# Second edge layer of a graph kernel: the softmax pieces two steps later, weighing and summing 14 and 16 steps behind the scores

## The reference

```python
# layer 0: attention with scores from Q and K
h = relu(layernorm(x))
Q, K, V = h @ Wq, h @ Wk, h @ Wv                       # 8 heads of 32
score = einsum('ehd,ehd->eh', K[src], Q[dst]) / sqrt(32) + edge_bias
attn  = softmax of score over the edges with the same dst
out   = segment_sum(attn * V[src], dst) @ Wp + bp
x     = x + layer_norm2(h1 + ffn(h1)),  h1 = layer_norm1(h + out)
# layer 1: attention with scores from two numbers per node and head
h = relu(layernorm(x)) @ W_lin + b_lin
feat = (h @ W_gat).reshape(N, 8, 32)
el, er = sum(feat * attn_l), sum(feat * attn_r)
e   = leaky_relu(el[src] + er[dst], 0.2)
a   = softmax of e over the edges with the same dst
out = leaky_relu(segment_sum(a * feat[src], dst) + gat_bias, 0.01)
x   = x + h + out
```

## Time and profile before

| | us |
|---|---|
| median of 3 runs | 7108.03 |
| lowest and highest | 7077.17, 7123.16 |
| the profiled execution | 7178.5 |
| its span, first to last instruction | 7176.6 |
| edge phase of layer 0 in it, about | 450 to 3150 |
| edge phase of layer 1 in it | 4276 to 6943 |
| mean granted TensorE clock in it, as a share of 2.4 GHz | 0.813 |

### The profile page before, as it was taken

One profiled execution on the slowest core, in us unless ns is written; L12 is line 12 of the kernel. 1 busy time (PEld: TensorE's weight loads), 2 busy tenths in 40 slices (PEclk: granted clock), 3 DMA queues, 4 the chain that ended last, 5 costly groups with the idle time before them and its releaser, 6 DMA issues. The chain is left out here.

```text
span 7176.6 us, 117024 instructions
## 1 busy us (share of the span) xinstructions
PE 5739.4 (80%) x24138; PEld 4403.4 (61%) x24138; DVE 4976.7 (69%) x12562; ACT 3482.2 (49%) x10958; POOL 3679.5 (51%) x4022
## 2 busy tenths in 40 slices
PE   8967777777777777779999948878788787888888
PEld 5545555555555555558999946666666666666666
DVE  4567888778888888886777736656566565665677
ACT  3356666666666666653333324444444444444440
POOL 1155555555555555534444455555555555655533
PEclk9978899889999999899999966666666666666669
DMA  5688888888988888872222235556556555665549
GB/s 182 202 248 268 271 280 279 266 264 280 286 274 272 274 271 278 264 235 80 85 85 85 84 105 167 165 162 166 168 163 168 161 161 162 170 166 163 163 142 296
DMA packets 849682, 1428.35 MB, mean 199 GB/s; under 512 B 123167, under 2 KB 628851, under 8 KB 849140
## 3 DMA queue, kind: packets, MB, share of 16 engines
q0 software_dynamic: 200192, 634.41, 31.1%
q1 hardware_dynamic: 543298, 511.88, 24.4%
q10 hardware_dynamic: 105650, 276.43, 10.0%
HBM read 1079.50 MB, written 342.73 MB: 198 GB/s over the span
## 5 line engine op out<-in xcount | busy, mean ns | idle before, releaser
L825 PE MATMUL bank<-ev,oh 128*128 128x264 f32 x7040 | 2557.0, 498 | 78.9 <-DVE ev L1284 60.6
L517 POOL DMA_INDIRECT Gf<-ft_tab,srcs x1564 | 1594.0, 1019 | 1154.7 <-DVE ev L1284 704.5
L517 POOL DMA_INDIRECT Gf<-kv_tab,srcs x1564 | 1508.0, 964 | 1308.7 <-DVE ev L1284 757.8
L825 PEld LDWEIGHTS bank<-ev,oh 128*128 128x128 f32 x7040 | 1619.8, 245 | 388.3 <-DVE ev L1284 88.3
L825 PE MATMUL bank<-qs,oht 128*128 128x256 f32 x3520 | 1077.3, 433 | 496.5 <-DVE prod L1193 245.5
L1284 DVE TENSOR_TENSOR ev<-Gf,ex 128x528 f32<-128x528 f32 x1760 | 1231.0, 699 | 2.1 <-ACT ex L686 1.3
L825 PE MATMUL bank<-Gf 128*128 128x128 f32 (+3 forms) x6284 | 1195.3, 343 | 4.5 <-ACT Gf L574 3.3
L825 PEld LDWEIGHTS bank<-qs,oht 128*128 128x128 f32 x3520 | 662.0, 209 | 770.9 <-issue 600.0
L614 ACT ACTIVATE absd<-lane,dlocs 128x128 f32<-128x128 f32 x3520 | 1112.8, 387 | 3.6 <-DVE bms L1159 3.5
L825 PEld LDWEIGHTS bank<-Gf 128*128 128x128 f32 x6284 | 936.1, 192 | 171.4 <-issue 98.7
L825 PEld LDWEIGHTS bank<-erq,oht 128*128 128x128 f32 x3520 | 735.1, 282 | 207.6 <-issue 157.7
(11 more groups left out here) (154 smaller groups left out, 5853.9 us busy)
## 6 DMA issues: line engine op xcount, KB each, us to landing
sums<-acc ACTq DMA_DIRECT2D x440, 528.0 KB
qs<-q_tab SPq DMA_DIRECT2D x880, 128.0 KB
oht<-dst_tab SPq DMA_DIRECT2D x880, 128.0 KB
qs<-dst_tab SPq DMA_DIRECT2D x880, 128.0 KB
Gf<-sums SPq DMA_DIRECT2D x196, 132.0 KB, 2.2
kv_tab<-Gf SPq DMA_DIRECT2D x98, 260.0 KB, 2.1
Gf<-in_x SPq DMA_DIRECT2D x196, 128.0 KB, 2.2
Gf<-kv_tab,srcs POOLq DMA_INDIRECT x1564
```

The lines of the kernel that those rows point to most:

```text
L517: pool.indirect_dma_start(out=rows[layer][:, m % SLOTS[layer], k, :], out_offset=None, in_=tab, in_offset=bass.IndirectOffsetOnAxis(ap=src ...
L825: return nc.tensor.matmul(o, a, r, start=first, stop=end)
```

## The change

In layer 1 alone (`LATE = (0, 2)`), the pieces of the softmax of block A move from steps 0 to 4 to steps 2 to 6 of the next turn, on DVE, ACT and PE. One piece stays: `scores_turned`, the transposition of S, is still in step 0. `links_turned` moves from step 5 to step 7, and the ACT part of the links from step 6 to step 0 of the turn after. Weighing and `agg` are 14 steps behind the scores in place of 12, `add` 16 in place of 14, and the stores 17 in place of 15. The ring of one-hots has twelve groups in layer 1; the two new ones lie in `prod`. One wait of ACT for its own `rm_made` is added, and the edge phase of layer 1 has one more turn at its end. Layer 0 keeps its order.

```diff
-OHG = 10
+OHG = (10, 12)
+BACK = (12, 14)
+LATE = (0, 2)
...
+        def group(B, g):
+            k = (B.n * 4 + g) % OHG[B.layer]
+            return oh[:, k, :, :] if k < OHG[0] else prod[:, k - OHG[0], :, :].rearrange("p k (a n) -> p (k a) n", n=P)
         def onehot(B, s):
-            return oh[:, (B.c * 4 + s // 2) % OHG, 2 * (s % 2):2 * (s % 2) + 2, :]
+            return group(B, s // 2)[:, 2 * (s % 2):2 * (s % 2) + 2, :]
...  ScalarE
-                wait(act, E_["agg"], B.c * ST + 2 * g + 2 - 2 * OHG)
+                wait(act, E_["agg"], B.c * ST + 2 * g + 2 - 2 * OHG[B.layer])
...
             def first_node(B):
+                if B.layer == 1:
+                    act.wait_ge(E_["rm_made"], B.c - 1)
...
-                        if s == 1 and A.live:
+                        if s == late + 1 and A.live:
                             row_values(A)
-                        if s == 2 and A.live:
+                        if s == late + 2 and A.live:
                             rescale(A)
-                        if s == 4 and A.live:
+                        if s == late + 4 and A.live:
                             factors(A)
-                        if s == 4 and B.live:
+                        if s == late + 4 and B.live:
                             link_rows(B)
-                        if s == 6 and B.live:
-                            links(B)
-                            if B.on(1).live:
-                                first_node(B.on(1))
+                        K, k = step_at(B, s - late)
+                        if k == 6 and K.live:
+                            links(K)
+                        if s == 6 and B.on(1).live:
+                            first_node(B.on(1))
...
-                        C, r = step_at(B, s - 15)
+                        C, r = step_at(B, s - BACK[layer] - 3)
...
-                for b in range(NB + 2):
+                for b in range(NB + 2 + layer):
...  TensorE (scores_turned(A) stays at s == 0)
-                        C, r = step_at(B, s - 12)
+                        C, r = step_at(B, s - BACK[layer])
                         if C.live:
                             agg(C, r)
-                        if s == 0 and A.live:
+                        if s == late and A.live:
                             row_values(A)
...  the same for columns, maxima_turned, rescale (1, 2, 3) and links_turned (5)
...  VectorE
-                        V_, v = step_at(B, s - 12)
-                        W_, w = step_at(B, s - 14)
+                        V_, v = step_at(B, s - BACK[layer])
+                        W_, w = step_at(B, s - BACK[layer] - 2)
...
-                        if s == 3 and A.live:
+                        if s == late + 3 and A.live:
                             below_maximum(A)
-                        if s == 6 and A.live:
-                            rescaled(A)
+                        if w == 0 and W_.live:
+                            rescaled(W_)
...
-                        if s == 0 and A.live:
+                        if s == late and A.live:
                             chunk_scans(A)
-                        if s == 2 and A.live:
+                        if s == late + 2 and A.live:
                             whole_scans(A)
...
-                        if s == 1 and A.live:
+                        if s == late + 1 and A.live:
                             row_scans(A)
```

More of the change, by code:

```diff
@@ L190, in build @@
         erq = sb("erq", [P, ST, H])
-        oh = sb("oh", [P, OHG, 4, P])
+        oh = sb("oh", [P, OHG[0], 4, P])
         oht = sb("oht", [P, ST, SPAN])
@@ L618, in onehots @@
                 act.wait_ge(E_["ohd"], 16 * B.c + 4 * g + 4)
-                wait(act, E_["agg"], B.c * ST + 2 * g + 2 - 2 * OHG)
-                act.activation(oh[:, (B.c * 4 + g) % OHG, :, :].rearrange("p c n -> p (c n)"),
+                wait(act, E_["agg"], B.c * ST + 2 * g + 2 - 2 * OHG[B.layer])
+                act.activation(group(B, g).rearrange("p c n -> p (c n)"),
                                absd[:, :, :].rearrange("p c n -> p (c n)"), ACT.Relu, scale=-1.0,
@@ L706, in edge_phase @@
             def edge_phase(layer):
-                at = {}
+                at, late = {}, LATE[layer]
                 def turn(B):
@@ L936, in edge_phase @@
             def edge_phase(layer):
+                late = LATE[layer]
                 def turn(B):
@@ L944, in turn @@
                             spread(layer, C, r)
-                        C, r = step_at(B, s - 12)
+                        C, r = step_at(B, s - BACK[layer])
                         if C.live:
                             agg(C, r)
-                        if s == 0 and A.live:
+                        if s == late and A.live:
                             row_values(A)
-                        if s == 1 and A.live:
+                        if s == late + 1 and A.live:
                             columns(A)
-                        if s == 2 and A.live:
+                        if s == late + 2 and A.live:
                             maxima_turned(A)
-                        if s == 3 and A.live:
+                        if s == late + 3 and A.live:
                             rescale(A)
-                        if s == 5 and B.live:
+                        if s == late + 5 and B.live:
                             links_turned(B)
@@ L1302, in edge_phase @@
             def edge_phase(layer):
-                at, landed = {}, {}
+                at, landed, late = {}, {}, LATE[layer]
                 def turn(B):
```

## The result

| | before | after |
|---|---|---|
| median of 3 runs, us | 7108.03 | 7010.25 |
| lowest and highest | 7077.17, 7123.16 | 7003.86, 7016.96 |
| the profiled execution | 7178.5 | 7010.25 |

The changed kernel takes 0.9869 of the time before, 95% interval [0.9838, 0.9899]: 98 us or 1.3% less. I had forecast 220 us. The sign is right, and the size is less than half of what I said. The forecast's own range, 6740 to 7040 us, takes 7010 in, since its upper end stands for only a third of the forecast gain.

What follows compares the result with a forecast made beforehand. The prediction took layer 1 to be bound by PE, starved at full clock by DVE's wait for the scan. 7178.5 - 225 + 5 = 6958.5 us profiled, or 7108 - 220 = 6888 us median; own range 6740 to 7040, whole range 6660 to 7130.

Steps and rivals of the forecast that it cites:

- PE, starved by DVE's wait for S: Layer 1's bound: PE idles 4.5 us per block, 3.4 us of it waiting for scans that DVE starts late.
- something I can't explain: At one block's scan, DVE starts 4.06 us after the transposition's record ends, though it waits for nothing else in the code.
- So the wait for a PE that is merely behind goes away: At `chunk_scans`, moved to step 2: DVE needs only what PE did two sums earlier; wait falls from 579.1 to under 100 us.
- I price a block in which PE never starves: Layer 1: 3.0 us per step at half clock, 2.4 at full, giving 22.3 us per block, 225 us less in all.
- the standstill moves: Rival, chance 0.25: PE's signals are held whatever DVE does, so waits move elsewhere; gain 0 to 0.5 us per block, 7080 us.
- the forecast's own rule: Layer 1's block is 24.0 us at half clock, less 0.25 us for each us at full clock.
- ACT's copies: ACT is busy for 44% of layer 1's stage, so its idle time covers the moved copies; costed at nothing.
- the ring: One-hot ring of twelve groups: margin between ACT and PE grows from two steps to four; nothing is paid.
- the later weighing: Slots are freed two steps later, gathers' lead shrinks from some 24 steps to 22; cost taken as zero.
- The full-clock rival: Rival, chance 0.12: PE, no longer starved, keeps 2.4 GHz for most of a block; 19.2 us per block, 6551 us.
- the slower one: Rival, chance 0.18: round trips meet a PE that is behind, so it idles later; 25.5 us per block, 7237 us.
- The drain of two steps: End of layer 1: two more steps drain after the last scores, 2 x 2.4 = 5 us.

Runs made afterwards that it cites:

- a_weigh_only: Changed kernel with the softmax pieces back at steps 0 to 4, only weighing, sums and ring moved, on a faster chip: 0.9998 of before, 18.86 us per block.
- set c: Runs on one slower chip, where the kernel before took 7107.58 us; the changed kernel repeated there took 7033.56 us, ratio 0.9891.
- The three controls: The changed kernel run again unaltered on three slower chips: 7023.49, 7033.56 and 7147.48 us, ratios 0.9899, 0.9891 and 0.9946 to the kernel before.
- c_weigh_only: Changed kernel with the softmax pieces back at steps 0 to 4, only weighing, sums and ring moved, on a slower chip: 1.0016 of before, 24.64 us per block.
- a_pause: Changed kernel with a memset that GpSimd waits for behind each pair of layer 1's gathers: 7378.54 us, ratio 1.0400, 27.45 us per block.
- a_half: Changed kernel with only the first of each span's two gathers in layer 1: 6460.32 us, 19.04 us per block.
- a_direct: Changed kernel with two plain loads of 128 rows in place of each span's two indirect gathers in layer 1: 6407.27 us, 18.72 us per block.
- c_busy: Changed kernel with plain loads in place of layer 1's gathers and two memsets behind each, keeping GpSimd busy: 6432.95 us, 18.91 us per block.
- after: The changed kernel as first profiled, against the kernel before: 7010.25 us, 0.9869 of the time before, 23.95 us per block of layer 1.

## Why the prediction was right in sign and wrong in size

**The bound.** "PE, starved by DVE's wait for S" described the trace but not its cause. I saw that a typical wait began with PE's backlog, and put the rest aside as something I can't explain. Against the rival I set that "the first 3 us of the wait are plain PE backlog". On a chip that holds no signal, the old order of these pieces has 104.1 us of waits there (a_weigh_only), about 1 us per block. PE is then busy for 93% of the stage, and GpSimd's gathers, at 1.32 us each for 14.2 per block, give 18.8 us per block where 18.86 was measured. Which of the two is the bound there isn't shown: with plain loads, which take GpSimd 559 ns, the block is still 18.7 us.

**The failed step** is what follows on "So the wait for a PE that is merely behind goes away", namely "I price a block in which PE never starves", with 22.3 us per block drawn from it. The wait at the scan did go, from 579.1 us to too little to be listed. But PE's idle time stayed, at 4.72 us per block, and the block is 23.95 us. DVE depends on PE at four points of a block's softmax and at two in every step, and a held signal stops it at whichever comes next. That is the rival "the standstill moves", which I gave 0.25, at the places that I had named for it: `add`, `el_er` (at `sred`) and `whole_scans`, together in 109 waits, one per block. Their longest are 5.0 to 7.1 us and their means 2.8 to 4.6 us. I sized it at 0 to 0.5 us per block, and 0.90 was measured (0.73 in set c). So the mechanism was the rival's, and the time lies between its price and the forecast's. POOL's wait for slots fell by 114 us, where I had named 200.

My line for being wrong was a block above 24 us. The three controls gave 24.12, 23.88 and 24.50, so the 23.95 of the first profile lies on it. That the time fell into the forecast's range is the width of the range and no support for its mechanism.

**What was gained** is PE's busy time, 1.09 us per block, less 0.19 us more of idleness. The same work was done at a mean clock of 0.68 in place of 0.64. Why the full clock lasts longer when the standstills fall in five places is not shown by any run. Had the forecast's own rule held (a quarter of a us back for each us at full clock), the rise of 0.04 in the clock, which is 0.08 x 24 = 1.9 us more at full clock, would give 0.5 of the 0.9 us; the rest is unaccounted for.

**The base.** The cut stage gave 24.36 us per block in place of 24.85. It made the forecast's gain 0.5 us per block smaller, so without this slip I would have been further off. That was luck.

**The other pieces.** ACT's copies, the ring, the added wait and the later weighing were costed at nothing. c_weigh_only confirms it for all but the copies (1.0016), for which there is no run. The full-clock rival did not happen (0.68, not 0.8), nor did the slower one, whose sign was a clock near 0.5. DVE does wait longer at `acc` for a PE that is behind, 116.6 us against 43.4 us in the whole stage before, but `acc` is none of the three round trips that this rival was about. At those the waits for a held signal cover what a backlog might add, so its mechanism is neither shown nor excluded. The drain of two steps is lost in the spread.

**What stays open:** what in the chip holds PE's signals, why two of five chips don't do it, and how many gathers in a row it takes. Runs of two with pauses (a_pause) and of at most four at half the number (a_half) held nothing; whether the length of the runs or their rate decides wasn't separated. The share of the indirect gathers in it is shown by a_direct and c_busy, each with layer 0 of the same execution beside it, and by a_half.

## What to carry to other kernels

A gap between the end of a producer and the start of a consumer that waits for nothing else is a cost of its own: price it first, and ask of a change how many other waits the same delay can reach. Slack given to one of six dependences between two engines moved such a delay here and gained only a part of it. Before reordering for a standstill, compare the profile with one of another chip, or with an experiment that takes the suspected disturber out; here that shows 5.4 us per block where the reordering got 0.9.

## What the runs showed of the hardware

- On the slower chips, in stages with real indirect gathers, PE's semaphore updates were often held and then came nearly together. In layer 1 of the kernel before, 194 waits of DVE and ACT ended 3.5 us in the mean and at most 8.4 us behind the end of PE's record; in `after` it was at most 12.4 us. Updates by DVE, ACT and GpSimd were not held (590 waits of `after`).
- The same program took 7094 to 7180 us on three chips and 6033 us on two. In layer 1 the durations of DVE's and GpSimd's instructions were equal (699 and 697 ns for a `weigh`, 1,027 and 1,023 ns for a gather), with a clock of 0.64 against 0.74. In layer 0 the window of a_weigh_only is 2357.80 us against 2734.70 in c_weigh_only, at a clock of 0.99 against 0.91:

```profile
406.40:2764.20 2357.80, 1885.12 (x8042) 1375.95 (x8042) 2271.33 (x4568) 1777.08 (x4869) 1584.35 (x1538) 0.99 0.98 321
```

```profile
431.60:3166.30 2734.70, 2050.01 (x8042) 1482.97 (x8042) 2277.56 (x4569) 1778.07 (x4869) 1483.00 (x1524) 0.91 0.87 275
```

- A plain load of 128 rows occupies GpSimd for 559 ns (a_direct), an indirect gather of the same bytes for 1,019 ns (after) and 0.30 us more until the next.
- GpSimd saw the semaphore of its own memset 1.0 us later, in 559 waits.
- With PE busy for 93% of layer 1 (a_direct) the granted clock was 0.73. The Trainium skill, page "TensorE: Matmul & The Clock Gate", section on HAM oscillation, says that an array kept fed stays warm. The trace agrees only in part: the clock rose from the 0.68 of the changed kernel, but a mean of 0.73 is still 1.2 GHz for about half of the time.
